# Batch loop of an attention and mixture-of-experts block reordered on all engines: four table slots, plain pieces in halves, a shorter prologue, the last 36 keys' products stacked

## The reference, cut to what matters

```
h = h + attn(layernorm(h))        # 12 heads, causal
h = h + moe(layernorm(h))         # 16 experts, capacity 64, top 1
# attn:
xn  = layernorm(x) * ln_w
Q   = xn[:, None] * W_qk[None, :, None]          # per head: an elementwise weight
P   = softmax(causal(Q @ Q.T / sqrt(192)))
V   = xn - mean(wte, axis=0)                      # wte is 50257 x 192
out = (P @ V) / arange(1, 165)                    # then heads side by side, @ W_o.T
```

## Time and profile before

| what | value |
|---|---|
| runs | 370.71, 372.57, 373.33 us, median 372.57 |
| the profiled execution | 372.14 us, of which the span is 370.4 us |
| TensorE busy | 332.7 us, 90% of the span |
| VectorE, ScalarE, GpSimd busy | 219.9, 127.9, 169.0 us |
| moved by DMA | 74.29 MB, mean 201 GB/s |
| chain that ended last | TensorE 39%, issue 18%, DMA 14%, GpSimd 14%, VectorE 8% |

### The profile page before, as it was taken

The page is one execution under the profiler, slowest core; times in us unless marked ns, Lnnn a source line. Parts: engine busy times, 40 slices in busy tenths (PEclk is TensorE's granted clock), DMA queues, the critical chain, the costliest instruction groups (busy, mean ns, idle before and its releaser), DMA issues.

```text
span 370.4 us, 6796 instructions
## 1 busy us (share of the span) xinstructions
PE 332.7 (90%) x2352; PEld 306.4 (83%) x2352; DVE 219.9 (59%) x546; ACT 127.9 (35%) x438; POOL 169.0 (46%) x181
## 2 busy tenths in 40 slices
PE   5886779999799899899899898999949999999992
PEld 1866679989699799799798798999824999999991
DVE  1479638678669679578588888656476222222221
ACT  2065423644643453454436004545720111111110
POOL 3067375583574763862953501450562134444321
PEclk9899889999999999999999999999998999999997
DMA  7399999899799899799797999900223599999930
GB/s 226 114 419 341 215 213 212 236 177 210 221 196 213 225 199 239 191 199 271 162 198 155 295 229 237 230 11 0 84 101 93 165 276 276 273 265 272 273 93 15
DMA packets 20176, 74.29 MB, mean 201 GB/s; under 512 B 3388, under 2 KB 9021, under 8 KB 18874
## 3 DMA queue, kind: packets, MB, share of 16 engines
q0 software_dynamic: 7344, 30.57, 40.8%
q1 hardware_dynamic: 9898, 40.40, 36.8%
q10 hardware_dynamic: 2912, 3.04, 2.9%
HBM read 66.12 MB, written 9.25 MB: 203 GB/s over the span
## 4 chain that ended last, share of the span: by engine, by line
PE 39%; issue 18%; DMA 14%; POOL 14%; DVE 8%; ACT 3%; POOLq 1%; SPq 0%; DVEq 0%; ACTq 0%
PE bO L1198 18%; DMA wbuf<-in_wte 11%; PE bE L1198 10%; PE bS L1198 5%; PE bJ L1198 4%; POOL AwA L390 4%; DMA H<-in_txtA 4%; POOL PA L416 3%; POOL wbuf L401 3%; POOL AwB L390 2%; ACT PA L552 2%; POOL PB L416 1%; DVE negmax L791 1%; PE bT L1544 1%; DVE PTB0L L808 1%
## 5 line engine op out<-in xcount | busy, mean ns | idle before, releaser
L552 ACT ACTIVATE PA<-bS,negmax 128x128 f32<-128x128 f32 x96 | 33.9, 366 | 85.2 <-DVE negmax L791 85.2
L416 POOL TENSOR_TENSOR PA<-PA,rn 128x512 f32<-128x512 f32 x24 | 25.8, 1075 | 64.3 <-DVE rn L803 64.3
L390 POOL TENSOR_TENSOR AwA<-zT,w 96x512 f32<-96x512 f32 x45 | 53.4, 1514 | 3.3 <-ACT zT L534 3.3
L1198 PE MATMUL bJ<-wo_sb,oTA 128*128 128x192 f32 x288 | 51.4, 328 | 0.0
L1198 PEld LDWEIGHTS bS<-zT,AwA 96*128 96x128 f32 x384 | 48.0, 197 | 1.1
L1198 PE MATMUL bS<-zT,AwA 96*128 96x128 f32 x384 | 48.2, 280 | 0.0
L1198 PEld LDWEIGHTS bJ<-wo_sb,oTA 128*128 128x128 f32 x288 | 46.2, 190 | 0.0
L1198 PE MATMUL bO<-PA,wx 96*128 96x112 f32 x384 | 45.4, 275 | 0.5 <-DVE PA L1171 0.5
L1198 PEld LDWEIGHTS bO<-PA,wx 96*128 96x128 f32 x384 | 44.9, 192 | 0.7 <-DVE PA L1171 0.7
L463 POOL DMA_INDIRECT out<-PA,yrow x16 | 15.0, 940 | 56.1 <-DVE PA L1187 56.1
L689 ACT ACTIVATE AwA<-bO 128x448 f32<-128x448 f32 x16 | 8.7, 543 | 78.4 <-PE bO L1198 52.8
(11 more groups left out here) (247 smaller groups left out, 690.9 us busy)
## 6 DMA issues: line engine op xcount, KB each, us to landing
wbuf<-in_wte POOLq DMA_DIRECT2D x20, 1344.0 KB, 13.0
wx<-in_wi SPq DMA_DIRECT2D x16, 576.0 KB
wx<-in_wo SPq DMA_DIRECT2D x16, 576.0 KB
wx<-in_wte SPq DMA_DIRECT2D x6, 1344.0 KB, 8.5
dispatched<-zeros SPq DMA_DIRECT2D x7, 675.5 KB, 10.3
wbuf<-in_wte SPq DMA_DIRECT2D x2, 1344.0 KB, 12.1
AwA<-dispatched ACTq DMA_DIRECT2D x14, 168.9 KB
wo_sb<-in_wo_attn SPq DMA_DIRECT2D x1, 1728.0 KB, 6.9
```

The costliest lines, as they stand in the source:

```text
L390: nc.gpsimd.tensor_tensor(o, zT[:, k, ss].unsqueeze(1).to_broadcast(list(o.shape)), w2[:, k, hs].unsqueeze(2).to_broadcast(list(o.shape)), ...
L416: nc.gpsimd.tensor_tensor(t, t, q.unsqueeze(2).to_broadcast(list(t.shape)), ALU.mult).then_inc(p_ready, 1)
L552: last = nc.scalar.activation(PA[:, h, :], bank[:, j * SA:(j + 1) * SA], ACT.Exp, bias=negmax[:, h:h + 1], accum_out=lsum[:, h:h + 1])
L1198: return nc.tensor.matmul(o, l, r, start=start, stop=stop, skip_group_check=True)
```

## The change

On every engine the order of the batch loop changes, and so do some buffers.

- **SP.** Patches and weights in halves of three blocks (`pat_in`, `pat2_in`); the text in two transfers, of 80 and of 12 partitions; `txtB` three times, stacked on 108 partitions (`SR`). Four first chunks instead of two; Wo between them. The plain chunks in two halves on two semaphores, begun once `tok_ready` is 5; `mat` behind them. The expert weights of all four slots wait for `acc_ready`, since slots 2 and 3 now hold table chunks.
- **Prologue.** The tokens of batches 0 and 1 are made as rows directly (`embed_rows`), and their statistics are taken one batch at a time. The rest of the embedding, its transposes and the statistics of batches 2 to 7 (`row_sums`, `variances`, `factors`) lie between the first scores and in the first iteration. The warm-up matmuls around the first z transposes are gone.
- **GpSimd.** `weigh` of round 0 comes ahead of the normalising of rounds 3 and 4; 18 adds over four slots, 2 or 3 a batch; the loop is written out six times. New: `last_keys` writes the last 36 keys of P three times side by side (108 columns), in two instructions.
- **ScalarE.** `zt_copy` ahead of `exps` 3 and 4; `t_copy(b, 3)` ahead of the next batch's first exponentials; `mat`'s copy moves from between iterations 1 and 2 into iteration 6.
- **TensorE.** `p_transpose(b, 2)` ahead of `value(b, 0)`; `p_transpose(b, 4)` waits for `last_keys`; the last 36 keys' three products become one with 108 stacked rows.
- **VectorE.** The table's total by contiguous additions (`slot_add`, `table_total`) in place of strided reductions.

The core of the diff:

```diff
-WBUF = 2
+WBUF = 4
-        plain = wx[0][:, :]
-        psums = wx[1][:, 0:WPLAIN * EMB]
+        wchunk = [wbuf[:, 0:WR * EMB], wbuf[:, WR * EMB:2 * WR * EMB], wx[2][:, :], wx[3][:, :]]
+        plain = [wx[0][:, h * HALF:(h + 1) * HALF] for h in range(2)]
...
+            for part, arrived in ((slice(0, 3), pat_in), (slice(3, 6), pat2_in)):
+                sp.dma_start(pw_sb[:, part, :], projw[:, part, :]).then_inc(arrived, 16)
+                sp.dma_start(pat_sb[:, part, :], patches[:, part, :]).then_inc(arrived, 16)
+            for p0, p1 in ((IMG, 116), (116, 128)):
+                sp.dma_start(H[p0:p1, 0:NBATCH, :], txtA[p0 - IMG:p1 - IMG]).then_inc(txt_in, 16)
...
+            def last_keys():
+                for q0 in (0, 2):
+                    t, k = PB[:, q0:q0 + 2, SEQ:SEQ + SR].rearrange("p q (t s) -> p q t s", t=3), PB[:, q0:q0 + 2, SA:SEQ]
+                    nc.gpsimd.tensor_tensor(t, k.unsqueeze(2).to_broadcast(list(t.shape)),
+                                            rn[0:HB * SB, 12 + q0:14 + q0].unsqueeze(2).unsqueeze(3).to_broadcast(list(t.shape)),
+                                            ALU.mult).then_inc(pb_ready, 1)
...
+            def iteration(b, chunks=()):
+                n = t_before(b, "z") + 1
+                weigh(b + 1, n, (0, 1), (0,))
+                normalise(b, range(3, SPR))
+                weigh(b + 1, n, (0, 1), (1,))
+                for c in chunks[0:1]:
+                    add_wte(c)
+                last_keys()
+                weigh(b + 1, n, (0, 1), (2,))
+                normalise(b + 1, (0,))
+                if is0(b):
+                    rsqrt(rstd[:, :, 2:NBATCH], nmr[:, :, 2:NBATCH], 3)
+                for c in chunks[1:2]:
+                    add_wte(c)
+                normalise(b + 1, (1,))
+                weigh(b + 1, n, (0, 1), (3,))
+                for c in chunks[2:3]:
+                    add_wte(c)
+                normalise(b + 1, (2,))
...
                 t_copy(b, 1)
-                exps(b, range(3, SPR))
                 if more:
                     zt_copy(t_before(b, "z") + 1, 1)
+                exps(b, range(3, SPR))
...
+            def slot_add(s, t):
+                for w in (s, t):
+                    dve.wait_ge(wte_in[w], slot_loads(w))
+                for r in (0, WR // 2):
+                    a, b = (chunk_rows(wchunk[w], r, r + WR // 2) for w in (s, t))
+                    last = nc.vector.tensor_tensor(a, a, b, ALU.add)
+                link(last)
...
             e_copy(b, 2)
-            plain_total()
-            slot_total(0)
+            slot_add(2, 3)
+            slot_add(0, 1)
+            slot_add(0, 2)
             residual_b(0)
-            slot_total(1)
+            table_total()
...
-                        mm(oo, vA[x][:, 0:E0], PTB0[y][:, :, :], i == 0, False)
-                        last = mm(oo, vB[x][:, 0:E0], PTB1[y][:, :, :], False, i == 2)
+                        last = mm(oo, vA[x][:, 0:E0], PTB0[y][:, :, :], i == 0, False)
+                if g == 3:
+                    last = mm(oo, vB[:, 0:E0], PTB1[:, :, :], False, True)
...
+                p_transpose(b, 2)
                 value(b, 0)
-                p_transpose(b, 2)
```

More of the change, by code:

```diff
@@ L282, in plain_loads @@
             def plain_loads(sp):
+                sp.wait_ge(tok_ready, 5)
                 for n in range(WPLAIN):
[L285 to L290, removed]
-            sp.dma_start(H[IMG:128, 0:NBATCH, :], txtA).then_inc(txt_in, 16)
+                    for h in range(2):
+                        if n:
+                            sp.wait_ge(plain_used, 4 * n - 2 + 2 * h)
+                        sp.dma_start(plain[h], wv[:, WCHUNKS - WPLAIN + n, h * HALF:(h + 1) * HALF]).then_inc(plain_in[h], 16)
@@ L380, in rsqrt @@
                                         ALU.pow).then_inc(pow_ready, 1)
-            rsqrt(rstd[:, :, 0:2], nmr[:, :, 0:2], 1)
+            for b in range(2):
+                rsqrt(rstd[:, :, b:b + 1], nmr[:, :, b:b + 1], b + 1)
             def weigh(b, n, ks, gs=range(4)):
@@ L445, in ffn_rsqrt @@
             def ffn_rsqrt(g):
                 k0, k1 = GROUPS[g]
-                rsqrt(rsq[:, :, k0:k1], var[:, :, k0:k1], 3 + g)
-            with pool.Fori(0, (NBATCH - 2) // 2) as i:
-                iteration(2 * i, i, 2)
-                iteration(2 * i + 1, i, 5)
-            iteration(NBATCH - 2, 0, None)
+                rsqrt(rsq[:, :, k0:k1], var[:, :, k0:k1], 4 + g)
+            for b in range(NBATCH - 2):
+                iteration(b, range(WBUF + 2 + 16 * b // 6, WBUF + 2 + 16 * (b + 1) // 6))
@@ L453, in _ @@
+            iteration(NBATCH - 2)
             normalise(LAST, range(3, SPR))
+            last_keys()
             ffn_rsqrt(0)
@@ L875, in _ @@
                                     w2[:, 0, :].unsqueeze(2).to_broadcast([EC, HEADS, SB]), ALU.mult).then_inc(awB0_ready, 1)
+            factors(1, 2, 2)
+            row_max(0, 0)
+            for j in range(2, 5):
+                add_patches(j)
+            row_factor(0, 0)
             row_max(0, 1)
-            row_factor(0, 0)
-            value_low(0)
+            row_sums(2, NBATCH)
             row_factor(0, 1)
             row_max(0, 2)
+            value_low(0)
             dve.wait_ge(t_ready, 1)
@@ L916, in iteration @@
                 dve.wait_ge(t_ready, t_before(b, "z") + 1)
+                if is0(b):
+                    factors(2, NBATCH, 3)
                 z(b + 2)
@@ L1213, in embed, with embed_rows @@
                 return last
+            def embed_rows(b, k0, k1):
+                for k in range(k0, k1):
+                    last = mm(bT[b][0:IMG, 0:EMB], pat_sb[:, k, b * IMG:(b + 1) * IMG], pw_sb[:, k, :], k == 0, k == 5)
+                if k1 == 6:
+                    last.then_inc(tok_ready, 1)
             def token_transpose(j):
-                bank = (bT[0], bE, bJ, bO[1])[j]
+                bank = (bE, bJ, bO[1])[j - 1]
                 for c in range(4):
@@ L1315, in value @@
                     for i, (x, y) in enumerate(SPLIT):
-                        first, final = odd == 0 and i == 0, odd == 1 and i == 2
+                        first, final = odd == 0 and i == 0, g < 3 and odd == 1 and i == 2
                         if g < 3:
```

305 lines of the change are left out of this document (148 added, 157 removed).

## The result

The changed kernel takes 368.06 us (median of seven runs) against 372.53 for the kernel before in the same series; the ratio is 0.990, with a 95% interval of 0.988 to 0.993. I had forecast 358.7 with a range of 351 to 365: a gain of 13.8 us, of which 4.5 came.

A forecast was written before the change was run, and what follows sets the result against it. TensorE and GpSimd were taken to bound the kernel after the first 60 us, not the DMA engines. Terms -3.5 - 6.6 + 0.5 - 0.4 - 10.0 + 5.5 + 1.5 - 0.8 = -13.8 gave 358.7 us, range 351 to 365.

The forecast's parts named there:

- The start: Up to the first P transposes: 27.2 us instead of 30.66, -3.5 (bounds 0 and -6).
- at the rates that wider transfers reach (412 GB/s): Loads at the start: some 2.9 MB in 7 us, landed at 10.5, z(0) at about 16.6 instead of 20.54.
- the three txtB copies take the engines: Rival on the start: it is not earlier, kernel at 362 us; chance 0.06.
- The first batch: First P transposes to next scores: 11.0 us instead of 17.60, -6.6; bounds -3 to -7.
- +0.5 (0 to 3): First batch: VectorE may wait for the plain chunk's halves, queued behind four chunks and Wo, +0.5 us (0 to 3).
- The steady period: Batch loop: period 24.5 us instead of 26.17, sum -1.66; six loop batches give -10.0.
- where I had 0.7: Steady period: GpSimd's first four heads' products before normalising remove a wait, net -0.7 us per period.
- +0.3: Steady period: last P transposes wait for `last_keys`, +0.3 us with the hop (bounds 0 and +2.4).
- The table's total: Last but one batch: VectorE's sums 13.46 to about 20 us, TensorE waits some 5.5 (bounds +0.6 and +9).
- my 1.5: After the stall at the table's total: TensorE's clock at its lower level for some microseconds, +1.5 us.
- 1.6 for 0.7: Table's mean to first expert product: forecast gain -0.7 us, from clock -1.5 and product +0.8.
- Behind the router the expert blocks fill TensorE; nothing there changes: Expert blocks, behind the router: TensorE filled, no change; forecast gain 0 to the end of the span.

The follow-up runs named there:

- e1: Changed kernel with txtB copies and statistics of batches 0 and 1 first, the other six batches' later: 375.29 us, ratio 1.008.
- g3: Changed kernel with variances(2, 8) early on VectorE and GpSimd's first two adds behind normalise(0, 0 to 2): 366.20 us, ratio 0.986.
- e8: Changed kernel with GpSimd's order undone, rounds 3 and 4 normalised ahead of the next batch's first products: 372.69 us, ratio 0.992.
- f2: Changed kernel with another, almost unused 1.5 MB tensor in device memory ahead of the tokens' one: 367.63 us in one run.
- e5: Changed kernel with an unused tile of 1280 bytes a partition in front of zT: 367.68 us, ratio 0.985.
- g1: Changed kernel loading only one sixth of the second weight matrix when an expert slot is refilled: 368.20 us, ratio 0.990.
- g2: Kernel before, loading only one sixth of the second weight matrix when an expert slot is refilled: 372.37 us, ratio 1.001.
- g5: One-sixth refill load of the second weight matrix, in f3 with further VectorE reordering (357.84 us without the omission): 357.42 us, ratio 0.958.
- f3: Changed kernel with txtA and txtB split, batches 0 and 1 first, variances(2, 8) early, first two adds behind normalise(0, 0 to 2): 364.20 us, ratio 0.982.
- e6: Changed kernel with variances(2, 8) ahead of value_low(0) and the first plain chunk summed behind row_factor(1, 2): 369.34 us, ratio 0.992.
- e3: Changed kernel with only variances(2, 8) moved on VectorE, to in front of value_low(0): 367.21 us, ratio 0.984.

## Why the prediction was wrong, step by step

**1. The start: wrong, and the largest miss (7.5 us).** The failed step is "at the rates that wider transfers reach (412 GB/s)": txtB landed at 15.1 us and not at 10.5, and z(0) came at 21.76 instead of 16.6. The runs showed 3.3 MB at 254 GB/s in the mean in its place, with 206 to 224 GB/s at full engines from 8 to 12 us and engines at 0.72 and less behind that; why they moved so little is open. e1 shows that this landing, with eight batches' statistics behind it, set z(0): splitting txtB took 4.9 us off. The stretch at a quarter of the engines is gone: the share is 0.97 at 8 to 10 us and still 0.72 at 12 to 14. The Trainium skill (DMA: Bandwidth & Descriptors, "Why a DMA increments its semaphore by 16 and not by 1") has a transfer run on the largest number of engines up to 16 that divides its slowest dimension, and so foretold that; the trace agrees, though no run here cuts txtA alone. But the change also loads txtB three times. I had this as a rival ("the three txtB copies take the engines", 0.06) and priced it at no gain. The price is a loss of 4.0: z(0) is 1.2 us later than before, and from there to the first P transposes it takes 12.9 us instead of 10.1, as TensorE's embedding of the second half lies between them at half clock (12 matmuls in 4.50 us).

**2. The first batch: direction right, "+0.5 (0 to 3)" for the plain halves mis-sized.** The 3.55 and 2.22 us of before went, and the next scores came as forecast. The wait for the plain chunk measured 3.1 to 3.6, at and beyond my upper bound. It was named and its cause too ("queued behind four chunks and Wo; two adds share the engines"); what I failed to do is to add up the bytes ahead of it. g3, with the adds behind, has the third batch 3.2 us earlier. I did not foresee that with the start mended this wait would grow to 11.8 (e1).

**3. The steady period: right, and better than said.** 24.12 against 24.5. The order of GpSimd is worth 0.5 (e8), where I had 0.7. No wait for `last_keys`, where I had +0.3, and GpSimd's products took 1.19 us in the mean instead of the 1.51 that I carried over from the earlier trace rows.

**4. The table's total: right in kind, sized half too high.** Sums of 17.9 us where I said 20 (13.46 before), a stall of 3.65 where I said 5.5. Two additions were slow beside GpSimd's products, 2.39 us and not 1.55, and the others ran when GpSimd had no product; most of the longer time is that four slots are more to add than two. An addition of 1344 elements took 1.55 by itself, which the 1.336 of 1152 elements gives by their number (1.56), where I had taken 1.45. The Trainium skill (GPSIMD Engine Reference, "Specifications") lists contention at the shared SBUF interfaces for VectorE instructions with two SBUF inputs; the two slow additions agree with it, and 1.7 us is what it cost here. The twelve matmuls behind the mean took 2.49 and 1.48 us instead of 1.55 and 0.81: 1.6 for the clock, near my 1.5. What the next stretch lost beyond the forecast (1.6 for 0.7) lies at the router, where 26 matmuls took 8.52 us instead of 7.20; they took 5.78 in f2 and e5, with the same instructions ahead of them, so that this is a difference between executions as well.

**5. "Behind the router the expert blocks fill TensorE; nothing there changes": wrong, 4.1 us in both profiles of the changed kernel, 0.8 to 4.8 in its relatives.** The row that warns of it is that the DMA engines are at 1.04 in that stage of the kernel before too. I read TensorE's 10.00 of 10.00 as a bound with room beside it. g1, g2 and g5 show that the waits end when less weight is loaded; why the weights come at some 250 instead of 265 to 277 GB/s, and why the stage took 85.4 us in one profile and 89.4 in another, is not settled.

The runs' median lies 3 us under the profiled execution (spans of the other executions 365.5 to 367.7 us). No trace shows those; the two things that varied by that much between profiles are the stage of step 5 and the clock at the router, and either may be smaller there.

## What to carry to other kernels

Before pricing an earlier start, add up all the bytes that every queue holds ahead of the first transfer that an in-order engine waits for, at the rate that these very transfers reach in the trace of before and not at the best rate in it, and ask which transfer binds next: mending the text alone made this kernel 6 us slower (e1), mending both made it 4 us faster (f3). A stage in which TensorE never waits may still stand on the edge of the DMA engines; look at their share there before calling it untouched, and take several profiles before pricing it. And when an in-order engine waits for a prefetch, bringing the transfer forward (g3) paid here, and moving the sums that wait for it to the end did not (e6).

## What was unexpected of the hardware

- A VectorE instruction on 128 x 12 elements, 0.17 us by itself, took 3.39 beside two GpSimd products; one on 128 x 128 took 2.75 in e6 beside another pair. Moved to where GpSimd was idle, or nearly so, the former cost nothing that can be seen (e3).
- DMA engines at a share of 0.97 moved 206 GB/s in one window of the start, with packets of 4.4 KB on the average. Four microseconds earlier they were at 1.07 and moved 389 GB/s with packets of 1.4 KB, and the table's chunks came at 432 GB/s with packets of 10.5 KB.
- The expert weights came at 241 to 257 GB/s in most windows of the changed kernels from 310 us on and at 265 to 277 in that of the kernel before, by the same transfers; an offset of 1280 bytes in SBUF and another 1.5 MB in device memory ahead did not bring the higher rate back, and the kernel before with longer code had 255 to 261.
- The same 26 matmuls took from 5.78 to 8.72 us at the router, by the level of TensorE's clock at that point.
